# Folding 64-wide layers onto both partition halves, and gathers with fixed index columns, in one pass of a graph network

## The reference, cut to what matters

```python
def _gin_conv(x, src, dst, wa, ba, wb, bb):
    agg = jax.ops.segment_sum(x[src], dst, num_segments=N_NODES)
    h = x + agg
    h = jnp.maximum(h @ wa + ba, 0.0)
    return h @ wb + bb
# layer 0: w1a is 128x64, w1b 64x64, w2a 64x256, w2b 256x256, wl 256x128
h = _gin_conv(x, src, dst, w1a, b1a, w1b, b1b)
h = jnp.maximum(h, 0.0)
h = _gin_conv(h, src, dst, w2a, b2a, w2b, b2b)
return h @ wl + bl
# around it: x = _layernorm(x + layer0(x)); then an RGCN, a GCN and three GAT layers likewise
```

## Time and profile before

| | |
|---|---|
| median of 3 runs | 4003.09 us (3991.21 to 4007.5) |
| profiled execution, its own time | 3992.48 us |
| its span, first to last instruction | 3990.8 us |
| weights and segments | 0 to 63.0 us |
| dense | 63.0 to 960.2 us |
| gin1 | 960.2 to 1314.9 us |
| all later phases | 1314.9 to 3990.8 us |
| mean granted TensorE clock | 0.887 of 2.4 GHz |

### The profile page before, as it was taken

The page is one execution under the profiler, slowest core; times in us unless marked ns, Lnnn a source line. Parts: engine busy times, 40 slices in busy tenths (PEclk is TensorE's granted clock), DMA queues, the critical chain, the costliest instruction groups (busy, mean ns, idle before and its releaser), DMA issues. The chain is left out here.

```text
span 3990.8 us, 83909 instructions
## 1 busy us (share of the span) xinstructions
PE 3108.9 (78%) x18931; PEld 2354.2 (59%) x18931; DVE 2677.1 (67%) x9706; ACT 2457.0 (62%) x6301; POOL 2365.2 (59%) x2776
## 2 busy tenths in 40 slices
PE   3999999993888799788768899366992778884662
PEld 2555555562444466444457689366992767784662
DVE  2888887784333466599958834388443888887873
ACT  1888887882222366566646667277661777774873
POOL 3777887776774677487677667500773017730766
PEclk9999999995999799899979999679995898885765
DMA  2556676752443244354446589355993669983441
GB/s 65 181 189 210 233 233 161 138 143 87 119 127 103 81 134 134 96 159 158 151 137 203 186 274 300 110 170 182 286 300 85 189 200 284 284 256 105 148 140 54
DMA packets 426874, 677.91 MB, mean 170 GB/s; under 512 B 80997, under 2 KB 161406, under 8 KB 426744
## 3 DMA queue, kind: packets, MB, share of 16 engines
q1 hardware_dynamic: 352344, 554.56, 43.8%
q0 software_dynamic: 74400, 121.87, 12.5%
HBM read 384.90 MB, written 295.47 MB: 170 GB/s over the span
## 5 line engine op out<-in xcount | busy, mean ns | idle before, releaser
L535 POOL DMA_INDIRECT msgs<-t_gat,row_i x600 | 577.3, 962 | 683.2 <-POOLq L123 486.9
L1651 PEld LDWEIGHTS n_p_q<-mean_col,n_sq 128*128 128x128 f32 x2352 | 308.5, 205 | 0.0
L1651 PE MATMUL n_p_q<-mean_col,n_sq 128*128 128x1 f32 x2352 | 298.3, 248 | 0.0
L2278 PE MATMUL a_p_t<-ident,a_wm 128*128 128x128 f32 x600 | 121.9, 337 | 199.4 <-DVE a_wm L2359 199.2
L2260 POOL DMA_INDIRECT out_rows<-a_res,a_stage x200 | 201.7, 1008 | 124.8 <-issue 84.4
L572 POOL DMA_INDIRECT t_where<-de_g_stage_id,de_g_stage_own x200 | 200.3, 1001 | 90.8 <-issue 51.4
L535 POOL DMA_INDIRECT msgs<-in_x,src_i x200 | 212.6, 1063 | 63.9 <-issue 63.9
L527 POOL DMA_INDIRECT g_g_rows<-t_where,g_g_stage x200 | 200.8, 1004 | 82.4 <-issue 47.6
L527 POOL DMA_INDIRECT g_ring<-t_h,g_g_stage x200 | 200.0, 1000 | 77.3 <-issue 48.2
L1490 PE MATMUL rg_p_b<-bases,rg_gt 128*128 128x512 f32 x400 | 207.2, 622 | 44.5 <-DVE rg_mg L1596 43.6
L1972 ACT ACTIVATE n_nt<-n_p_t,cxt 128x512 f32<-128x512 f32 x294 | 200.1, 681 | 62.2 <-PE n_p_t L1946 62.0
(11 more groups left out here) (394 smaller groups left out, 9462.2 us busy)
## 6 DMA issues: line engine op xcount, KB each, us to landing
n_h<-t_gat SPq DMA_DIRECT2D x294, 264.0 KB
t_gat<-n_hn SPq DMA_DIRECT2D x196, 264.0 KB
t_x<-de_x SPq DMA_DIRECT2D x196, 256.0 KB
a_h<-t_gat SPq DMA_DIRECT2D x150, 264.0 KB
t_gat<-a_hn SPq DMA_DIRECT2D x100, 264.0 KB
t_gat<-de_h SPq DMA_DIRECT2D x98, 264.0 KB
g_xd<-t_xd SPq DMA_DIRECT2D x100, 256.0 KB
n_x<-t_x SPq DMA_DIRECT2D x98, 256.0 KB
```

Of the source, the lines that this page charges most:

```text
L535: self.nc.gpsimd.indirect_dma_start(out=self.msgs[:, c, 0:width], out_offset=None, in_=table, in_offset=bass.IndirectOffsetOnAxis(ap=idx[: ...
L1651: last = self.nc.tensor.matmul(p_q[:, j:j + 1], sq[:, j * D:(j + 1) * D], self.mean_col[:], start=True, stop=True)
L2278: t = nc.tensor.transpose(p_t[:, w, j * D:(j + 1) * D], wm[:, w, j, :], self.ident[:])
```

## The change

In the weights phase the 64-wide weights are laid out for both halves of the partitions: `w1b2` is a 128x128 tile with `w1b` twice on its diagonal and zeros elsewhere, `w2a2` holds `w2a` in partitions 0 to 63 and again in 64 to 127, and the biases are doubled likewise. That makes 26 small loads instead of 22, and two small memsets.

In the dense phase the first 256 nodes of a group have their 64 hidden features in partitions 0 to 63 and the last 256 nodes in 64 to 127, so `ha` and `ht` are 128x256 instead of 64x512. `p_a` becomes two products that write the two halves of the partitions, `p_b` one product with 256 columns, the transposes of `ht` two of 128x128 instead of four of 64x128. The w2a layer becomes four products of 256 columns (two output halves `t`, two node halves `b`), where node half `b` reads partitions 64b to 64b+63 and writes bank `b` of a two-bank PSUM tile `p_c`. They are issued in one piece ahead of `p_a`, where `second(0)` was; `second(1)`'s place behind `p_a` is empty. The two rectifications read across both banks, and the semaphores `pe_c` and `act_c` count once a group.

On POOL, `slot_gathers` and `map_gathers` are unrolled fully, with fixed index columns, without staging copies and hardware loops. The ring store follows two groups later (`lag = 2`). All scatters count on one semaphore that is awaited once at the end. `map_gathers` writes into `row_i` directly, which is first filled with one memset.

```diff
-        stage_x = sb("g_stage_x", [128, UN, G4], I32); stage_own = sb("g_stage_own", [128, UN, G4], I32)
-        stage_id = sb("g_stage_id", [128, UN, G4], I32)
-        lag = 1
+        lag = 2
         self.resident_gather(self.src_i, a["x"], D, got, bounds_check=N - 1, oob_is_err=False)
-        steps(pool, AG, lag, rows)
-            nc.gpsimd.tensor_copy(stage_own[:, u, :], self.own_i[:, bass.ds(i * G4, G4)]).then_inc(staged_map, 1)
-            nc.gpsimd.tensor_copy(stage_id[:, u, :], self.slot_id[:, bass.ds(i * G4, G4)]).then_inc(staged_map, 1)
-            self.hold(pool, (staged_map, 2 * i + 2))
-        steps(pool, AG, 0, owners)
+        for i in range(AG + lag):
+            if i < AG:
+                u = i % UN
+                if i >= UN:
+                    self.hold(pool, (stored[u], 16 * (i // UN)))
+                for j in range(G4):
+                    nc.gpsimd.indirect_dma_start(
+                        out=ring[:, u, j, :], out_offset=None, in_=a["x"],
+                        in_offset=bass.IndirectOffsetOnAxis(ap=self.dst_i[:, i * G4 + j:i * G4 + j + 1], axis=0)).then_inc(arrived[u], 16)
+            if i >= lag:
+                n = i - lag
+                pool.wait_ge(arrived[n % UN], 16 * G4 * (n // UN + 1))
+                pool.dma_start(self.slots(self.xd, n // UN, n % UN), ring[:, n % UN]).then_inc(stored[n % UN], 16)
+        for c in range(CHUNKS):
+            nc.gpsimd.indirect_dma_start(
+                out=self.where, out_offset=bass.IndirectOffsetOnAxis(ap=self.own_i[:, c:c + 1], axis=0),
+                in_=self.slot_id[:, c:c + 1], in_offset=None, bounds_check=N - 1, oob_is_err=False).then_inc(mapped, 16)
...
     def map_gathers(self, pool, sb, sem):
-        steps(pool, AG, lag, step)
+        nc.gpsimd.memset(self.row_i[:], SLOTS).then_inc(blank, 1)
+        for c in range(CHUNKS):
+            nc.gpsimd.indirect_dma_start(
+                out=self.row_i[:, c:c + 1], out_offset=None, in_=self.where,
+                in_offset=bass.IndirectOffsetOnAxis(ap=self.src_i[:, c:c + 1], axis=0),
+                bounds_check=N - 1, oob_is_err=False).then_inc(self.map_taken, 16)
...
-                    def second(t):
+                    def second():
                         if live(k, u, 1, DG):
-                            wait(pe, s["act_c"], 2 * i - 3 + t)
-                            nc.tensor.matmul((p_c0, p_c1)[t][:], self.w2a[:, t * D:(t + 1) * D], ht[:],
-                                             start=True, stop=True).then_inc(s["pe_c"], 1)
+                            wait(pe, s["act_c"], i - 1)
+                            for t in range(2):
+                                for b in range(2):
+                                    m = nc.tensor.matmul(p_c[:, b, t * 256:(t + 1) * 256], self.w2a2[b * H:(b + 1) * H, t * D:(t + 1) * D],
+                                                         ht[b * H:(b + 1) * H, :], start=True, stop=True)
+                            m.then_inc(s["pe_c"], 1)
...
-                        nc.tensor.matmul(p_b[0:H, :], self.w1b[:], ha[:], start=True, stop=True).then_inc(s["pe_b"], 1)
+                        nc.tensor.matmul(p_b[:, 0:256], self.w1b2[:], ha[:], start=True, stop=True).then_inc(s["pe_b"], 1)
...
-                        for j in range(G4):
-                            m = nc.tensor.transpose(p_b[:, j * H:(j + 1) * H], ht[:, j * D:(j + 1) * D], self.ident[0:H, 0:H])
+                        for n in range(2):
+                            m = nc.tensor.transpose(p_b[:, n * D:(n + 1) * D], ht[:, n * D:(n + 1) * D], self.ident[:])
...
-                        nc.tensor.matmul(p_a[0:H, :], self.w1a[:], xt[:], start=True, stop=True).then_inc(s["pe_a"], 1)
-                    second(1)
+                        for b in range(2):
+                            m = nc.tensor.matmul(p_a[b * H:(b + 1) * H, 0:256], self.w1a[:], xt[:, b * 256:(b + 1) * 256], start=True, stop=True)
+                        m.then_inc(s["pe_a"], 1)
...
-                        nc.scalar.activation(ht[:], p_b[0:H, :], ACT.Relu, bias=self.b1b[:]).then_inc(s["act_b"], 1)
+                        nc.scalar.activation(ht[:], p_b[:, 0:256], ACT.Relu, bias=self.b1b2[:]).then_inc(s["act_b"], 1)
```

More of the change, by code:

```diff
@@ L551, in rows @@
[L551 to L560, removed]
@@ L582, in slot_gathers @@
         pool.wait_ge(got, 16 * CHUNKS)
+        pool.wait_ge(mapped, 16 * CHUNKS)
     def map_gathers(self, pool, sb, sem):
         nc = self.nc
-        rows = sb("g_rows", [128, UN, G4, 1], I32); stage = sb("g_stage", [128, UN, G4], I32)
-        arrived = [sem(f"g_arrived{u}") for u in range(UN)]
-        staged, taken, blank = sem("g_staged"), sem("g_taken"), sem("g_blank")
-        self.map_taken = taken
-        lag = UN - 1
-        nc.gpsimd.memset(rows[:].rearrange("p a b o -> p (a b o)"), SLOTS).then_inc(blank, 1)
@@ L593, in map_gathers @@
-        pool.wait_ge(blank, 1)
-        def step(k, u):
-            def freed(k, u):
-                return ((taken, UN * k + u - UN + 1),)
-            if live(k, u, 0, AG):
-                self.gather_group(pool, k, u, AG, self.src_i, stage, staged, self.where, rows, 1, arrived, freed,
-                                  bounds_check=N - 1, oob_is_err=False)
-            if live(k, u, lag, AG):
-                v = (u - lag) % UN
-                kk = k - (1 if u < lag else 0)
-                pool.wait_ge(arrived[v], 16 * G4 * (kk + 1))
-                nc.gpsimd.tensor_copy(self.row_i[:, bass.ds((UN * kk + v) * G4, G4)],
-                                      rows[:, v].rearrange("p j o -> p (j o)")).then_inc(taken, 1)
@@ L613, in norm_part @@
+        pool.wait_ge(self.map_taken, 16 * CHUNKS)
     def norm_part(self, part, rows, st, mv, inv, chain):
@@ L664, in phase_dense @@
             inv2 = sb("inv2", [128, UN, G4]); rs2 = sb("rs2", [128, UN, G4]); nb2 = sb("nb2", [128, UN, G4])
-            p_x, p_a, p_b, p_c0, p_c1, p_o = (ps(n) for n in ("p_x", "p_a", "p_b", "p_c0", "p_c1", "p_o"))
+            p_x, p_a, p_b, p_o = (ps(n) for n in ("p_x", "p_a", "p_b", "p_o"))
+            p_c = ps("p_c", (128, 2, 512))
             p_h = ps("p_h", (128, 2, 512))
@@ L797, in step @@
                         wait(act, s["pe_b"], i)
-                        nc.scalar.activation(ha[:], p_a[0:H, :], ACT.Relu, bias=self.b1a[:]).then_inc(s["act_a"], 1)
+                        nc.scalar.activation(ha[:], p_a[:, 0:256], ACT.Relu, bias=self.b1a2[:]).then_inc(s["act_a"], 1)
                     rectify(1)
```

59 lines of the change are left out of this document (28 added, 31 removed).

## The result

The changed kernel takes 3940.4 us (median of 20 runs, 3930.9 to 3996.1) against 3997.1 us for the kernel before in the same rounds (20 runs, 3987.4 to 4038.6): ratio 0.986, 95% interval 0.9841 to 0.9878, or 56.6 us by the medians. Some executions run slower at a lower granted clock (three of these 20, at 0.853 to 0.855 where the others have 0.858 to 0.880); they count in the medians and not in the ratio. The forecast was 3952 (3925 to 3983). Its likeliest case was a gain of 34 to 55 us, and 55 to 65 was called "more than forecast": the profiled execution lies in the first, the medians just inside the second.

A forecast was written before the change was run, and what follows sets the result against it. POOL's list of 600 indirect transfers was taken to bound the dense phase. Scatters 43.5 plus ring 5.0 less weights 2.5 gave 46.0 us off, so 3946.5 from the profiled run or 3957.1 from the median; middle 3952, range 3925 to 3983.

The forecast's parts named there:

- likeliest case: Whole program: POOL sets the end of the dense phase, gain 34 to 55 us; chance 0.67.
- more than forecast: Rival: interference goes, or the 10.4 us at the dense phase's end shrink; gain 55 to 65 us, chance 0.10.
- POOL's list bounds the dense phase: Dense phase: POOL's 600 indirect transfers, not the 97% busy PE, set when gin1 begins.
- Scatters 43.5: POOL's scatter groups: two copies and their wait cost 0.87 us a group; 50 groups give 43.5 us.
- Ring 5.0: POOL's ring groups: the staging copy costs 0.10 us each; 50 groups give 5.0 us; the last wait remains.
- Interference as before: POOL's gathers of about 1.32 instead of 1.0 us: same total expected, between 14 us gain and 12 us loss.
- Weights 2.5: Weights phase: four more loads on SP at 0.63 us each lose 2.5 us; the memsets cost nothing.
- The 10.4 us at the end: Dense phase, from last scatter to the instruction behind the barrier: called landing and barrier, with no engine working.
- PE's step: Dense phase: step falls from 8.28 us to 7.73, or 6.2 if halves run together, with DVE's floor 7.09.
- The slower rival: PE's dense step: changing partition half drains the array; step 9.37 us, program about 4068 us; chance 0.07.
- So what PE gains, 54 to 117 us, is worth nothing here: Dense phase: PE ends at 811 to 874, before POOL's 904, so its gain only lengthens POOL's time alone.
- gin1: Phase after the dense one: map_gathers loses copies, but other work hides it; nothing gained, still 355 us long.

The follow-up runs named there:

- e6_move64_again: Changed kernel with the last 64 of the 200 resident gathers moved from the dense phase into gin1; 3865.8 us, ratio 0.9697 to the kernel before.
- e9_one_input: Changed kernel with DVE's longest step operation taking one tensor and a scale instead of two tensors, GCN bias left out; 3940.7 us, ratio 0.9863.
- e11_constant: Changed kernel with DVE's longest step operation using constant 1.5 for the per-partition scale, bias left out; two runs, 3953.2 and 4013.1 us.
- e5_pool_only_again: Kernel before with only the new slot_gathers and map_gathers on POOL, PE's side unchanged; 3974.9 us, ratio 0.9949.
- e10_more_loads: Changed kernel with eight more small loads ahead of the 26 in the weights phase; 3946.6 us (1 run).
- e7_fold_only_again: Changed kernel with the old slot_gathers and map_gathers, so only the fold (layout on both partition halves) remains; 3995.3 us, ratio 1.0019.
- e8_same_half_first: Changed kernel with the four w2a products reordered so those of one array half follow each other; 3939.4 us, ratio 0.986.

## Why the prediction held, and where it didn't

**POOL's list bounds the dense phase: right.** After the change PE, DVE and ACT do nothing for 90 us before gin1, and e6_move64_again gets 85 of them back by taking work off that list.

**Scatters 43.5: right, 42.9.** They are 1.29 us apart once the pipeline is done, as the spacing inside a group had shown: 5.16 us for four, where the old group takes 6.0. Throughout, as the prediction had it, they are not: beside the pipeline 31 of 132 take longer, and the mean is 1.38.

**Ring 5.0: right in kind, 8.1.** The stores at the end are 5.6 apart and the last wait stayed. The rest is interference, as below.

**Interference as before: mis-sized.** The term stood at 0 within -12 to +14, because the number of dense steps doesn't change. The resident gathers, whose code didn't change, gained 6.3 us: 1063 to 1028 ns. Counting each transfer's excess over its kind's median, the three parts carried 13.2, 6.9 and 3.7 us before and 5.6, 3.5 and 5.6 after. The fold does it, not the POOL code: the resident part has 6.0 with the fold alone and 12.9 with the POOL part alone. For the scatters it is the other way round: 11.6 with the POOL part alone and 3.1 with the fold alone, since without the copies more of them meet the pipeline, as the prediction feared. By what means stays open. The long transfers start beside DVE's L864 more than 3 times as often as its share of the time (58 of 81 in 19% of it), yet changing its second input or its scale brings nothing (e9_one_input, e11_constant).

**Weights 2.5: plausible, not decided.** The first product of DVE starts at 20.13 before and 20.22 after, 0.1 us later. With the same 22 loads it starts at 17.91 in e5_pool_only_again, and with 26 at 19.8 to 20.8 in six executions, 1.9 to 2.9 later. Four loads by the 0.55 of e10_more_loads are 2.2. But the two executions with 22 loads differ by 2.2 us themselves, as much as the term.

**The 10.4 us at the end: named wrongly.** The prediction took them for "landing and barrier". After the change the last scatter has landed at 893.9, 1.3 us behind the end of its instruction. So landing is the small part. Most of the rest is one instruction of POOL's sequencer, here of the kernel before and then of the changed one (three times its duration in ns, then its start):

```profile
L655 POOLq DRAIN  x1: 7902/7902/7902, 951.3 to 951.3; - x1
```

```profile
L632 POOLq DRAIN  x1: 7159/7159/7159, 894.0 to 894.0; - x1
```

**PE's step: right, at the far end of the range given.** 7.73 and 6.2 were the two cases for PE and 7.09 DVE's floor; the halves run side by side, and DVE sets the step beside the gathers. The end comes near what was worked out for that case: PE's last work at 804 and DVE's at 808, for 811. In part this is luck: 7.09 is not a floor, as the steps beside the resident gathers take 6.7 us (it left out what DVE idled otherwise), and the steps beside the scatters, at 8.75, make up for it. The slower rival, a drain at each change of half, is refuted by the same rows: it had the w2a product at over 2.1 us, and it takes 1.07. (Its 12 records by 0.14 us are 1.68, not 1.64; nothing hangs on it.)

**"So what PE gains, 54 to 117 us, is worth nothing here": wrong.** This is the step that failed. It holds after the list has been shortened only because PE has been too. The prediction's own numbers had it: POOL at 904, PE at 925 without the fold. e5_pool_only_again shows it, with a gain of 20 us and 35.7 us between POOL's last scatter and gin1. The fold's share of the 56.6 is thus some 37 us, while alone it gives nothing measurable. The forecast of the whole didn't suffer, as both parts were in it.

**gin1: right.** 353.9 against 354.7 us.

**The sum.** Forecast 46.0. Measured at gin1's start 58.1: 42.9 + 8.1 + 6.3 + 0.9 for the shorter end, less 0.1 at the start. About 9 of the 12 us between are interference (24 us of excess before, 15 after), which the forecast had in its range and as a part of "more than forecast"; 2.4 are the weights term, which this pair of profiles doesn't show, and 0.9 the end. The 6.5 us lost in the later phases came out of it again, which brought the profiled execution nearer to the forecast by chance. They have the same code and a clock of 0.86; e6_move64_again has 2678.2 there and e5_pool_only_again 2689.4, so this is a spread between executions and was not followed further.

## What to carry to other kernels

When a phase ends with the later of two independent chains, work out the end of each chain for each part of a change, alone and together: a part that is worth nothing alone can be what makes the other's gain count. Look then whether the chain that ends last has work that a later phase needs first, and move it to where that engine idles; here that gave more than the change itself. Read a list of software-issued transfers by the spacing of its starts: two index copies of 0.2 us each and their wait cost 0.86 us a group of four here.

## What the runs showed of the hardware

- Two 32-bit matmuls with 64 rows on different partition halves run at once, and so do two with 64 columns: 1024 columns in 1.07 us, 512 in 0.58. The order of issue doesn't matter within one product (1.08 in e8_same_half_first).
- At the end of the dense phase POOL's DRAIN takes 7.2 us with the new list (the changed kernel, e5_pool_only_again, e6_move64_again) and 7.9 with the old one (the kernel before, e7_fold_only_again), although the last transfer has landed; those of the other engines there take 0.007 to 2.2 us. At the end of other phases of the kernel before POOL's takes 4.1 to 17.0 us (0.6 in the weights phase). What sets its length isn't known.
- A one-input operation of DVE with a constant runs its four pieces in 0.62 us where two inputs take 1.12, and the ring gathers beside it are hit harder: 60 of 200 long, by 0.42 us each, where the changed kernel has 17, by 0.13. The resident gathers are not (1024 ns in the mean, 1028 in the changed kernel). The Trainium skill (SBUF — State Buffer, Who interferes with whom) says that such an operation in its faster mode takes a port that POOL needs, for the whole instruction. The ring of e11_constant agrees with it in sign, its resident gathers don't bear it out, and that DVE was in that mode isn't shown.
- In one lot the pipeline nearly stood still while POOL issued its transfers: PE was busy 27 of 200 us, the kernel before took 5538 us, and a list with fewer pauses made it slower, ratio 1.059. What may be a mild form of it shows in the changed kernel: PE's steps take 8.75 us beside the scatters and 6.7 beside the resident gathers (8.8 and 8.2 in the kernel before). Why that is wasn't tested.
